# Grouped attention as one unrolled line of 128 steps, values weighed half a unit in every step

## The reference

```
q = rms_norm(h @ Wq, q_norm_w)        # h = layernorm(x); 16 heads of 128
k = rms_norm(enc @ Wk, k_norm_w)      # 4 key heads of 128, 1601 encoder rows
v = enc @ Wv                          # each key head serves 4 query heads
probs = softmax(q k^T / sqrt(128))
y = (probs @ v) @ Wo                  # x = x + y
```

## Time and profile before

| | |
|---|---|
| runs | 2007.18, 2012.59, 2012.29 us, median 2012.29 |
| profiled execution | 2008.84 us, its span 2007.0 us |
| mean granted TensorE clock | 0.955 of full speed |
| grouped attention | 660 to 1922 us of the span |
| busy in the whole span | PE 1739.7, DVE 1303.9, ACT 980.6, POOL 615.8 us |

### The profile page before, as it was taken

One profiled execution on the slowest core, in us unless ns is written; L12 is line 12 of the kernel. 1 busy time (PEld: TensorE's weight loads), 2 busy tenths in 40 slices (PEclk: granted clock), 3 DMA queues, 4 the chain that ended last, 5 costly groups with the idle time before them and its releaser, 6 DMA issues. The chain is left out here.

```text
span 2007.0 us, 32922 instructions
## 1 busy us (share of the span) xinstructions
PE 1739.7 (87%) x10769; PEld 1524.8 (76%) x10772; DVE 1303.9 (65%) x2618; ACT 980.6 (49%) x2010; POOL 615.8 (31%) x482
## 2 busy tenths in 40 slices
PE   5787599999999589998989998989998979999944
PEld 4777578888888578887878887878887868888832
DVE  3444377777776567667656677757677657676667
ACT  3333133333333255655545555545655545555536
POOL 1111054445444323223213222222222232222115
PEclk8888699999999799999999999999999999999969
DMA  3100011111110221011120100020110101010120
GB/s 103 38 33 0 21 46 39 39 39 39 39 39 14 75 65 35 17 25 23 29 56 25 28 24 25 17 69 17 25 35 17 25 22 30 14 19 17 12 76 22
DMA packets 78826, 66.90 MB, mean 33 GB/s; under 512 B 14264, under 2 KB 74208, under 8 KB 78688
## 3 DMA queue, kind: packets, MB, share of 16 engines
q1 hardware_dynamic: 78688, 65.14, 12.1%
HBM read 64.01 MB, written 1.11 MB: 32 GB/s over the span
## 5 line engine op out<-in xcount | busy, mean ns | idle before, releaser
L1420 DVE TENSOR_TENSOR ga_pT<-ga_ps_t,ga_pT 128x512 fp32r<-128x512 f32 (+1 forms) x512 | 293.0, 585 | 153.3 <-ACT ga_pT L1282 151.6
L1282 ACT ACTIVATE ga_pT<-ga_ps_t 128x512 fp32r<-128x512 f32 (+1 forms) x512 | 253.7, 518 | 206.7 <-PE ga_ps_t L1531 204.8
L1576 PE MATMUL ga_ps_m<-ga_pT,ga_v 128*128 128x512 f32 (+1 forms) x832 | 318.9, 415 | 4.6 <-DVE ga_pT L1420 4.6
L1468 PE MATMUL ga_ps_s<-ga_kT,ga_qT 128*128 128x400 f32 (+1 forms) x1536 | 313.9, 353 | 8.5 <-ACT ga_probs L1303 4.3
L1531 PE MATMUL ga_ps_t<-all_eye,ga_probs 128*128 128x128 f32 (+1 forms) x1664 | 266.4, 277 | 37.8 <-DVE ga_pT L1420 18.5
L1468 PEld LDWEIGHTS ga_ps_s<-ga_kT,ga_qT 128*128 128x128 f32 x1536 | 273.9, 189 | 15.2 <-ACT ga_probs L1303 9.0
L1303 ACT ACTIVATE ga_probs<-ga_ps_s,ga_neg_max 128x1200 f32<-128x1200 f32 (+1 forms) x256 | 238.4, 931 | 50.9 <-DVE ga_neg_max L1437 50.9
L1531 PEld LDWEIGHTS ga_ps_t<-all_eye,ga_probs 128*128 128x128 f32 (+1 forms) x1664 | 197.7, 140 | 80.5 <-DVE ga_pT L1420 32.8
L1578 PE MATMUL ga_ps_m<-ga_pT,ga_v 128*128 128x256 f32 (+1 forms) x832 | 233.4, 281 | 0.0
L1468 PE MATMUL ga_ps_t<-ga_w_in,ga_encT 128*128 128x256 f32 (+1 forms) x1248 | 176.6, 291 | 50.8 <-DVE ga_pT L1420 31.4
L1432 DVE TENSOR_REDUCE ga_part_max<-ga_ps_s 128x1 f32<-128x1200 f32 x128 | 179.5, 1402 | 47.0 <-PE ga_ps_s L1468 47.0
(11 more groups left out here) (222 smaller groups left out, 2693.0 us busy)
## 6 DMA issues: line engine op xcount, KB each, us to landing
ga_w_in_raw<-in_L_xattn_Wq SPq DMA_DIRECT2D x16, 512.0 KB, 5.3
ga_w_out_raw<-in_L_xattn_Wo SPq DMA_DIRECT2D x16, 512.0 KB, 4.6
ga_inv_rows<-ga_inv_row SPq DMA_DIRECT2D x64, 128.0 KB, 3.6
ca_cache<-in_ctx SPq DMA_DIRECT2D x4, 1536.0 KB
ga_enc<-in_ctx SPq DMA_DIRECT2D x4, 1536.0 KB
ex_raw<-in_L_ffn_Wg SPq DMA_DIRECT2D x32, 96.0 KB, 1.9
ex_raw<-in_L_ffn_Wu SPq DMA_DIRECT2D x32, 96.0 KB, 2.0
ex_raw<-in_L_ffn_Wd SPq DMA_DIRECT2D x32, 96.0 KB, 2.0
```

Source lines behind the costliest of these rows:

```text
L1282: last_one = nc.scalar.activation(dst(HI), src, ACT.Copy, scale=scale)
L1420: ins = nc.vector.tensor_tensor(dst(LO), src, f32(dst(HI)), ALU.subtract)
L1468: mm = nc.tensor.matmul(out, lhs(a), rhs(c), start=first and n == 0, stop=last and n == 2)
L1576: nc.tensor.matmul(ps_m[:, :, :], values[0:top, HI, tile, :], pT[0:top, :, tile, :], start=tile == 0, stop=False)
```

## The change

The loop over rows goes. One plan of N = 128 steps for all rows and DRAIN = 4 steps behind them is written out; nothing drains between rows, and the steps of the next row follow at once. Every step now has the same shape on PE: scores, two `pT` jobs, "early" preparing, half a unit of weighing, two more `pT` jobs, "late" preparing. The `pT` jobs are turned unit by unit, tiles 0 to 7 of both steps of a unit in one step (two steps later than the first of them), tiles 8 to 12 in the next, hence the third `probs` buffer. An odd step weighs 8 tiles, an even one 5.

The preparing is laid out anew: `q` in steps 0 and 1 with `q_eps` at the end of step 1, `qT` 0 early in step 2, `kv` spread over steps 2 to 6, all four `kT` in step 7, `y` in two halves in steps 4 and 5. ACT now reads the first two jobs, makes both exponentials, and then reads the rest. The result of a unit is scaled in an odd step, before that step's `q_eps` or `k_eps` on POOL. The query and the output weights share one raw tile `w_raw`, so each load of one waits for the split of the other; the encoder comes in four pieces through two buffers. The sum, the shapes and the number of all matmuls, copies and remainders are the same, but that `y` is read in two halves of 128x256.

The core of the diff:

```diff
+    def turned_probs(n):
+        if n % 2 == 0:
+            u, order = n // 2 - 1, [(0, 0), (1, 0), (0, 1), (1, 1)]
+        else:
+            u, order = (n - 3) // 2, [(0, 2), (0, 3), (1, 2), (1, 3)]
+        return [("pT", (t, k), u) for t, k in order] if 0 <= u < UNITS else []
+    def weighed(n):
+        u, half = ((n - 3) // 2, 0) if n % 2 else (n // 2 - 2, 1)
+        return [("weigh", half, u)] if 0 <= u < UNITS else []
+    def prepared(n):
+            early, late = {
+                0: ([("q", 0, to)], []),
+                1: ([("q", 1, to)], [("q_eps", 0, to)]),
+                2: ([("qT", 0, to)], [("qT", 1, to), ("kv", 0, to)]),
+                3: ([("kv", 1, to)], [("kv", 2, to)]),
+                4: ([("kv", 3, to), ("k_eps", 0, to)], []),
+                5: ([], [("kv", 4, to)]),
+                6: ([("kv", 5, to)], [("kv", 6, to), ("k_eps", 1, to)]),
+                7: ([("kT", 0, to), ("kT", 1, to)], [("kT", 2, to), ("kT", 3, to)])}[s]
+        if 0 < g <= GROUPS and s in (4, 5):
+            late = [("y", s - 4, g - 1)] + late if s == 4 else late
+            early = [("y", s - 4, g - 1)] + early if s == 5 else early
+        if at == 0 and row < B:      # row, at = divmod(g + 2, G)
+            late = late + {6: [("norm", 0, row)], 7: [("xT", 0, row), ("encT", 0, row), ("encT", 3, row)]}.get(s, [])
...
+        return ([("scores", 0, n)] if n < N else []) + turns[0:2] + early + weighed(n) + turns[2:4] + late
...
-        probs = [sb(f"probs{i}", [P, KV]) for i in range(2)]
+        probs = [sb(f"probs{i}", [P, KV]) for i in range(PB)]
...
+            # SP, before the steps
+            sp.wait_ge(w_q_lo, 1)
             load_out(0)
+            sp.wait_ge(w_out_lo, 1)
             load_q(1)
...
+            # ACT, before the steps (POOL has the same three)
+            split_out(0)
+            split_q(1)
+            split_kv(1)
...
+            # ACT, step n
+                for e in jobs:
+                    if e[0] != "weigh":
+                        ring(e)
+                    if turns and e == turns[1] and n < N:
                         exp(n, 0)
+                        exp(n, 1)
+                    if turns and e == turns[2] and n % 2 == 0 and 0 <= n // 2 - 2:
+                        take_low_part(n // 2 - 2)
...
+            # DVE
+            for n in range(N + DRAIN):
+                if n % 2 == 0 and 0 <= n // 2 - 1 < UNITS:
+                    invert(n // 2 - 1)
+                if n % 2 and 0 <= (n - 5) // 2 < UNITS:
+                    add_parts((n - 5) // 2)
+                if n < N:
+                    largest(n)
+                for e in plan[n]:
+                    entry(e)
```

More of the change, by code:

```diff
@@ L859, in grouped_attention @@
     blocks = [(k * WIDE, COLS_EVEN if k == NB - 1 else (k + 1) * WIDE) for k in range(NB)]
-    assert all((z - a) % 2 == 0 and z - a <= BANK for a, z in blocks)
+    assert all((z - a) % 2 == 0 and 0 < z - a <= BANK for a, z in blocks)
     key_tiles = [range(0, 4), range(4, 8), range(8, 12), range(12, 13)]
-    JOBS = len(key_tiles)
-    RING = ("xT", "encT", "q", "kv", "qT", "kT", "pT", "y")
[L868 to L907, removed]
@@ L928, in grouped_attention @@
+    plan = {-1: prologue}
+    for n in range(N + DRAIN):
+        plan[n] = step_plan(n)
+    RING = ("xT", "encT", "q", "kv", "qT", "kT", "pT", "y")
+    place, read_place = {}, {}
+    for n in range(-1, N + DRAIN):
+        for e in plan[n]:
+            if e[0] in RING:
+                assert e not in place
+                place[e] = len(place)
+                if e[0] != "y":
+                    read_place[e] = len(read_place)
     with ExitStack() as ctx:
         r = Room(nc, ctx, "ga")
-        sb, ps, sem, counted = r.sb, r.ps, r.sem, r.counted
@@ L988, in grouped_attention @@
[L988 to L998, removed]
-        empty = counted("empty", BODY, before=PRO)
-        scores = counted("scores", N_STEPS * NB)
@@ new lines, in grouped_attention @@
+        var_ready = sem("var_ready")
+        rstd_ready = sem("rstd_ready")
+        xn_ready = sem("xn_ready")
+        squares = sem("squares")
+        q_eps = sem("q_eps")
+        q_scaled = sem("q_scaled")
+        q_normed = sem("q_normed")
+        k_eps = sem("k_eps")
+        k_scaled = sem("k_scaled")
+        k_normed = sem("k_normed")
+        full = sem("full")
+        read = sem("read")
+        empty = sem("empty")
+        scores = sem("scores")
+        maxed = sem("maxed")
@@ new lines, in _ @@
+            split_kv(0)
+            act.wait_ge(qk_ready, 1)
+            for e in prologue:
+                if e[0] == "xT":
+                    split_q(0)
+                if e[0] in RING:
+                    ring(e)
+            split_out(0)
+            split_q(1)
+            split_kv(1)
+            for n in range(N + DRAIN):
+                g, s = n // STEPS, n % STEPS
+                jobs = [e for e in plan[n] if (e[0] in RING and e[0] != "y") or e[0] == "weigh"]
+                turns = turned_probs(n)
+                if not turns and n < N:
+                    exp(n, 0)
+                    exp(n, 1)
+                for e in jobs:
+                    if e[0] != "weigh":
+                        ring(e)
+                    if turns and e == turns[1] and n < N:
@@ L1462, in _ @@
-            rows(dve, body)
+            dve.wait_ge(cleared, 4)
+            for e in prologue:
+                entry(e)
+            for n in range(N + DRAIN):
+                if n % 2 == 0 and 0 <= n // 2 - 1 < UNITS:
+                    invert(n // 2 - 1)
+                if n % 2 and 0 <= (n - 5) // 2 < UNITS:
+                    add_parts((n - 5) // 2)
+                if n < N:
+                    largest(n)
+                for e in plan[n]:
+                    entry(e)
         @block.tensor
@@ L1574, in weigh @@
+            def weigh(half, u):
+                k_first, k_last = halves[half]
+                pe.wait_ge(*emptied(("pT", (QT - 1, k_last), u)))
+                if half == 0 and u:
+                    pe.wait_ge(u_here, u)
+                values = v[u // HG % 2]
+                for k in halves[half]:
                     for tile in key_tiles[k]:
```

833 lines of the change are left out of this document (388 added, 445 removed).

## The result

The changed kernel takes 2018.7 us (median of 8 runs, 2016.7 to 2021.8), the kernel before 2012.4 beside it (8 runs); the ratio is 1.0033, 95% interval 1.0018 to 1.0048. So it is slower, by about a third of a per cent: little, but the interval lies clear of 1. The profiled execution took 2018.7 us, its span is 2016.8, the mean granted clock 0.944 (before 0.955).

The account below looks back on a forecast made before the run. PE, 87% busy, was taken as the limit, yet waiting 9 us per 72.6 us group. Terms +27, -24, +9, -5, -4, +3 gave +6 on the profiled 2008.8, plus 3.5 for the median: 2018 us, range 1970 to 2045.

Parts of the forecast that it names:

- Steps of a plain group: Eight steps of a group, priced one by one from old durations: 73.5 us against 72.6 before, without the clock term.
- C: Rival: ACT and DVE always free banks in time, only the POOL wait stays; 67.5 us a group, about 1920 us; chance 0.16.
- The new wait: Step 2: `qT` 0 waits for POOL's scaled queries because `q_eps` now ends step 1; 2.8 us idle in 15 groups.
- The clock: Clock drops near the 2.8 us idle time of each group: 1.0 us a group, from 0 to 1.6, up to 3.
- D: Rival: waits pile up, a second clock drop per group and DVE late into the maximum; 2045 us; chance 0.22.
- Changes of row: Three row changes: no drain, but encoder jobs and `norm` remain; 12 us each against 20, -24 in all.
- Group 0: First group: ACT's first exponential waits for a chain of loads and splits; step 0 12 to 14 us, +9.
- Prologue: Start of the stage: first encoder piece is a third of the row, but norm weights load last; -4 us (0 to -7).
- End: Drain at the end of the stage, one step longer: +3 us.
- The last group: Group with nothing to prepare: pairs of steps of 11.6 us instead of 13.9, with `y` 43 instead of 48.2; -5.
- B: Rival: the clock stays up behind the 2.8 us gap and the start costs half; 1999 us (1988 to 2006); chance 0.2.
- E: Rival: half units do not cover the ring, even steps stay as before; some 2030 us; chance 0.42 shared with the main forecast.

Follow-up runs that it names:

- qt_later: Changed kernel with the two `qT` jobs moved from step 2 to step 3, `kv` 0 and 1 into step 2: 1982.7 us against 2018.7.
- exp_split: Changed kernel with ACT reading the first early job between the two exponentials instead of behind both: 1995.3 us against 2018.7.
- kt_earlier: Changed kernel with `kT` 0 moved from step 7 to the end of step 5, behind `kv` 4: 2006.4 us against 2018.7.
- kt_one_six: Fastest kernel (several edits combined, 1912.4 us) with `kT` 1 moved from step 7 to step 6, ahead of `kv` 6: 1919.7 us.
- norm_split: Changed kernel with `norm` in two parts, statistics at the end of step 5, scaling at the end of step 6: 2011.4 us against 2018.7.
- start: Changed kernel with group 0's output weights loaded and split in step 7, as in other groups, not ahead of the steps: 2014.9 us against 2018.7.
- norm_first: Changed kernel with norm weights loaded first and the first query weights split ahead of `kv` 0: 2015.7 us against 2018.7.

## Why the prediction held, point by point

**Steps of a plain group.** Priced 6.9, 7.4, 11.6, 9.5, 9.4, 8.9, 8.7, 11.1, sum 73.5; measured 7.08, 7.45, 11.66, 9.47, 9.40, 8.88, 8.65, 10.94, sum 73.53. The walk through the ring with durations of the earlier trace rows gave each step within 0.2 us. Wait by wait the trace shows less than was priced, 7.6 us in group 4 instead of 9.9, in part because a row counts idle time from the end of the matmuls it reports (scores 2.44 us), while the prediction counted from start to start (2.28). This walk is what made C unlikely, and C did not come.

**The new wait.** Priced 2.8 us, in 15 groups, 40 in all; measured 2.6 in 14 groups, 1.6 in group 0 and 0.8 ahead of the steps, 38.6 in all. `qt_later` shows its worth, -36 us: 28 in idle time, as other waits of the ring grew, and 6 with the clock, in groups 1 to 14. It also shows that a later `qT` removes it; no run changed POOL's speed. One link of the walk was wrong though its number was right: the prediction hangs `q_eps` at 16.1 on ACT's late reading of `q` 1, but with that reading 0.67 us sooner it comes no sooner (`exp_split`); the two `pT` jobs ahead of it, turned behind the weighing, set it.

**The clock.** Priced 1.0 us a group; eight plain groups measure 73.5 to 75.3, mean 74.54, so 1.0. The mechanism was only half right. Windows of one microsecond in groups 4 and 13, each behind the wait for POOL (the last three figures are granted clock, DMA share, GB/s):

```profile
1032.00:1033.00 1.00, 1.00 (x7) 0.92 (x8) 0.00 (x0) 0.69 (x3) 0.00 (x0) 1.00 0.00 0
```

```profile
1728.00:1729.00 1.00, 1.00 (x5) 0.98 (x5) 0.00 (x0) 0.24 (x3) 0.00 (x0) 0.50 0.00 0
```

```profile
1727.77 1.09 PE L1500 MATMUL ga_ps_t<-all_eye,ga_qn 128*128 128x128 f32 x4 [2.58 <-POOL ga_qn L1199]
```

An idle time of 2.60 us brings no drop in group 4, one of 2.58 us brings one in group 13. Other groups drop in step 0, behind step 7's several short waits (1.24, 0.87 and 0.77 us ahead of 1085.05):

```profile
1086.00:1087.00 1.00, 1.00 (x4) 0.99 (x4) 0.00 (x0) 0.40 (x1) 1.00 (x1) 0.50 0.08 1
```

I had that only in D, as a second drop in each group; in fact five of eight plain groups have one drop, in one place or the other, of 1.3 to 1.6 us, and three have none. The rule of the Trainium skill (TensorE: Matmul & The Clock Gate, "Why this matters for your kernels") is not enough here: the longest idle time in a plain group, 2.60 us, stays below its length, and the clock drops. What decides whether a given group drops stays open; `kt_earlier` and `kt_one_six` show that a shorter step 7 is not enough.

**Changes of row.** Priced 12 us each, measured 12.4; the drain and its `y` went, and DVE's wait for POOL of 2.13 us (priced 3) with the maximum behind it came. `norm_split` confirms that wait as the main cost of step 7.

**Group 0.** Priced +9, measured +5.5. Step 0 was right (12 to 14 against 12.45) and `start` shows its cause; the rest of the group was mis-sized, as its first steps have no `pT` jobs yet and step 1 lasts 5.70 us.

**Prologue.** The failed term: -4, measured +1.0. What I counted came: from the stage's first instruction to the end of the encoder's transposes the kernel after needs 16.0 us, the one before 20.0, norm weights included. What the sum left out is the way from there to the first scores: 29.9 us instead of 24.9. The late split of the query weights (a wait of 4.38 against 1.50) is in it, and `norm_first` gets back 2.6 us there.

**End.** +3 and +3.2. The last group: -5 and -4.0.

**Sum.** +6 in the prediction, +10 measured between two profiled executions. I added 3.5 us for the median of before over its profiled execution; the profiled execution of after lies on its own median, so two errors of 4 us cancel, and 2018 against 2018.7 is closer than the working was. Of the rivals: B needs all plain groups near 73.5 us without a drop, and three of eight are so; C needs 67.5, and D two drops in each group: neither is in the trace. E is refuted as well: in the last group pairs last 11.8 us (5.73 and 6.11) instead of 13.9, so the halves do cover the ring.

## What to carry to other kernels

Walk a new order of work through every queue, step by step, with durations of the old trace: for the ring that gave eight steps within 0.2 us. Where a producer's last stage (here 3.9 us of POOL) lies between two jobs, leave room for it (here two steps instead of one: -36 us), look also at what stands ahead of its first stage in that engine's own order, and fix the largest wait first, since edits elsewhere may pay only then. A rewrite of structure and order is two changes: apart they were -18 and +24 us. And a move that frees one wait can hold up a transfer which merely stands behind it in the queue (24 us here).

## What the runs showed of the chip

DVE's instruction on 8 elements of each partition, `k_sq_eps`, takes 2.24 us at 684.74 in the rows of the prologue, and ends with POOL's instruction on 1024 elements that began 0.13 us ahead (both at 686.95 to 686.98). Where the query weights are split earlier, in the kernel with the norm weights first, the same instruction takes 0.17:

```profile
684.26 0.17 DVE L1367 TENSOR_SCALAR ga_k_sq_eps<-ga_k_sq 128x8 f32<-128x8 f32 x1
```

In step 1 of group 4 `q_sq_eps` takes 0.47 and ends at 1028.12, again as POOL's instruction before it (L1218) ends; in group 0, where POOL does nothing at that time, it takes 0.17. The Trainium skill (SBUF — State Buffer, "Terms") says that VectorE and GpSimd share a pair of ports that one of them holds for its whole instruction; by that rule, the trace agrees. A small step of DVE on a critical chain is not small beside a long one of POOL.

The second surprise is the clock: with the same order of work and the same idle times, neighbouring groups differ by some 1.5 us, and which of them drop changes from kernel to kernel.
